# A fused attention and expert-FFN layer: the LoRA rows' transposes move one tile later, and a small product of the shared LoRA takes rounded operands

## What is computed

```
xn  = layernorm(x)
Q,K = elu(xn @ wq.T + bq) + 1, elu(xn @ wk.T + bk) + 1;  V = xn @ wv.T + bv      (16 heads of 32)
att = (Q @ (K^T V)) / (Q . sum(K) + 1e-8) @ wo.T + bo                            (linear attention)
w   = two best of 8 experts by sigmoid(xn @ W_router) + expert_bias, normalised
gate, up = xn @ W + (xn @ sA) @ sB / 8 + sum over experts of w_e (xn @ A_e) @ B_e / 8
hidden   = silu(gate) * up                                                        (1376 wide)
out = x + att + hidden @ W_down + (hidden @ sA_down) @ sB_down / 8 + experts' down LoRA
```

## Time and profile before

| | |
|---|---|
| median of the runs | 669.27 us |
| the profiled execution: its time, its span | 669.42 us, 667.6 us |
| PE matmuls busy | 659.3 us (99%) |
| DVE / ACT / POOL busy | 56% / 39% / 19% |
| granted TensorE clock | 1.000 of full speed |
| chain that ended last, by engine | PE 94%, DVE 3%, DMA 1%, ACT 1% |

### The profile page before, as it was taken

One profiled execution on the slowest core, in us unless ns is written; L12 is line 12 of the kernel. 1 busy time (PEld: TensorE's weight loads), 2 busy tenths in 40 slices (PEclk: granted clock), 3 DMA queues, 4 the chain that ended last, 5 costly groups with the idle time before them and its releaser, 6 DMA issues.

```text
span 667.6 us, 10326 instructions
## 1 busy us (share of the span) xinstructions
PE 659.3 (99%) x3568; PEld 545.4 (82%) x3568; DVE 376.3 (56%) x698; ACT 257.8 (39%) x413; POOL 127.1 (19%) x290
## 2 busy tenths in 40 slices
PE   7999999999999999999999999999999999999998
PEld 6899998877767788888888888888888888888886
DVE  6677888778676955434355443445344326534433
ACT  5434444566326323332343333243233324333321
POOL 3565676627336320000000000000000000000000
PEclk9999999999999999999999999999999999999999
DMA  6876665743745669930025000021400001300001
GB/s 215 311 256 212 214 235 194 261 183 149 292 170 196 236 183 3 77 128 0 1 79 221 32 0 0 0 75 72 184 0 0 0 8 71 127 0 0 0 0 63
DMA packets 41643, 74.21 MB, mean 111 GB/s; under 512 B 19393, under 2 KB 20289, under 8 KB 39953
## 3 DMA queue, kind: packets, MB, share of 16 engines
q1 hardware_dynamic: 38672, 64.52, 34.2%
q10 hardware_dynamic: 2736, 9.05, 3.4%
q0 software_dynamic: 208, 0.30, 0.3%
HBM read 52.81 MB, written 21.04 MB: 111 GB/s over the span
## 4 chain that ended last, share of the span: by engine, by line
PE 94%; DVE 3%; DMA 1%; ACT 1%; issue 0%; POOL 0%; DVEq 0%; POOLq 0%
PE bank L1246 21%; PE bank L1248 21%; PE bank L1247 21%; PE bank L1491 18%; PE bank L1464 6%; DVE den L1092 2%; PE bank L1477 1%; PE bank L1475 1%; PE bank L1265 1%; PE bank L1277 1%; DMA w_raw<-in_wkT 1%; PE bank L1364 1%; PE bank L1502 1%; PE bank L1504 1%; PE bank L1286 0%
## 5 line engine op out<-in xcount | busy, mean ns | idle before, releaser
L1246 PE MATMUL bank<-x,up_h 128*128 128x512 f32 (+1 forms) x352 | 137.1, 389 | 0.2 <-DVE x3r L1057 0.2
L1247 PE MATMUL bank<-x,up_h 128*128 128x512 f32 (+1 forms) x352 | 137.0, 389 | 0.0
L1248 PE MATMUL bank<-x,up_l 128*128 128x512 f32 (+1 forms) x352 | 137.0, 389 | 0.0
L1183 DVE TENSOR_TENSOR hf<-bank,silu 128x512 f32<-128x512 f32 x44 | 30.4, 691 | 155.0 <-issue 135.3
L1491 PE MATMUL bank<-dn,hid_h 128*128 128x512 f32 x352 | 108.8, 390 | 0.0
L677 ACT ACTIVATE hid_h<-hf 128x512 fp32r<-128x512 f32 x44 | 27.8, 632 | 144.1 <-DVE hf L1183 144.1
L1246 PEld LDWEIGHTS bank<-x,up_h 128*128 128x128 f32 x352 | 66.1, 188 | 14.4 <-issue 0.7
L1491 PEld LDWEIGHTS bank<-dn,hid_h 128*128 128x128 f32 x352 | 65.8, 188 | 14.5 <-DVE res L1208 0.6
L1248 PEld LDWEIGHTS bank<-x,up_l 128*128 128x128 f32 x352 | 66.1, 188 | 13.8
L1247 PEld LDWEIGHTS bank<-x,up_h 128*128 128x128 f32 x352 | 66.1, 188 | 13.7
L888 DVE TENSOR_TENSOR up_l<-up_raw,up_h 128x1024 fp32r<-128x1024 f32 x44 | 55.0, 1250 | 28.1 <-ACT up_h L677 28.1
(11 more groups left out here) (166 smaller groups left out, 1082.9 us busy)
## 6 DMA issues: line engine op xcount, KB each, us to landing
x<-scr_x SPq DMA_DIRECT2D x7, 2048.0 KB, 8.5
up_raw<-in_ffn_up SPq DMA_DIRECT2D x11, 768.0 KB, 7.4
scr_x<-xt ACTq DMA_DIRECT2D x16, 512.0 KB, 4.7
xin<-in_x SPq DMA_DIRECT2D x16, 256.0 KB, 4.9
scr_z<-zt SPq DMA_DIRECT2D x16, 256.0 KB, 2.1
x3r<-in_x SPq DMA_DIRECT2D x16, 256.0 KB, 3.1
scr_att<-x3r SPq DMA_DIRECT2D x16, 256.0 KB, 2.8
z<-scr_z SPq DMA_DIRECT2D x4, 1024.0 KB, 4.8
```

Of the source, the lines that this page charges most:

```text
L1183: nc.vector.tensor_tensor(hf[:], ps_u[:], silu[:], ALU.mult).then_inc(h_done, 1)
L1246: nc.tensor.matmul(dst, lh, rh, start=start, stop=False, **kw)
L1247: nc.tensor.matmul(dst, lh, rl, start=False, stop=False, **kw)
L1248: return nc.tensor.matmul(dst, ll, rh, start=False, stop=stop, **kw)
```

## The change

1. LoRA transposes. PE's `lora_transposed(t-2)` at the end of tile t becomes `lora_transposed(t-3)` directly behind tile t's `transpose_tokens(t+1)` (in tile 15, which has none, behind k). ACT's `lora_out(t-3)` comes behind the rounding of va, before the wait for `zraw`; DVE's `lora_lo(t-3)` comes behind `kf`, before `normalise(t+2)`. Tile 15 does two: pair 12 in the new place, and pair 13 at its end as before. SP stores each pair one tile later, so the store of pair 12 moves behind `x3_load(1)` and the load of `sa_dn`. Four tiles instead of two stand unrolled before the loop.
2. shared_down. The host puts sA_down and sB_down three times into each strip of 32 rows (24 rows of data). ACT rounds both (128x384 and 128x512) between queries(0,(2,)) and queries(0,(3,)), DVE turns the rows of one copy of each into remainders with two masks, and PE multiplies the rounded operands in one float32r matmul per chunk (the three copies give h.h, l.h and h.l).
3. `sa_r` and `sb_r` lie where later data go, so SP's loads of the up weights 8 to 10 and ACT's first `split_up` wait for the last shared_down (`sh_ready` 11).

```diff
 tiles:
-            body(0, 0, 0)
-            body(1, 0, 1)
-            with eng.Fori(0, SPLIT_FROM // 2 - 1) as p:
+            for t in range(4):
+                body(t, t // 2, t % 2)
+            with eng.Fori(2, SPLIT_FROM // 2) as p:
...
 SP:
             sp.dma_start(w_raw[:, 0], dram["woT"]).then_inc(s2_in, 16)
-            store_z(0)
...
             sp.dma_start(w_raw[:, 1], dram["wqT"]).then_inc(s2_in, 16)
-            store_z(1)
+            store_z(0)
...
                 if t < TILES - 1:
-                    store_z(t - 2)
+                    store_z(t - 3)
...
-            for t in range(TILES - 3, TILES - 1):
+            for t in range(TILES - 4, TILES - 1):
                 store_z(t)
...
             att_store(GROUPS - 2, True)
+            sp.wait_ge(sh_ready, FC)
             for c in range(WQ_CHUNK, FC):
 ACT:
                 round_to(vf[:, s, 0:KD - 1, :, 0:DK], ...).then_inc(va_done, 1)
+                if behind(t, 3):
+                    lora_out(t - 3)
...
-                if behind(t, 2):
+                if isinstance(t, int) and t == TILES - 1:
                     lora_out(t - 2)
...
-            queries(0, (2, 3))
+            queries(0, (2,))
+            act.wait_ge(sa_in, 16)
+            act.wait_ge(s2_in, 16 * STAGE2_LOADS)
+            act.wait_ge(vz_ready, TILES)
+            round_to(sa_r[:], sa_dn[:])
+            round_to(sb_r[:], sb_dn[:]).then_inc(shr_done, 1)
+            queries(0, (3,))
...
+            act.wait_ge(sh_ready, FC)
             split_up(0, 0, 0)
 DVE:
                 nc.vector.scalar_tensor_tensor(kf[:, s, :], ...).then_inc(kf_done, 1)
...
+                if behind(t, 3):
+                    lora_lo(t - 3)
                 if ahead(t, 2):
                     normalise(t + 2, s)
...
-                if behind(t, 2):
+                if isinstance(t, int) and t == TILES - 1:
                     lora_lo(t - 2)
...
             sub(bdn[0:ER, 1], bdn_raw[0:ER, 1], bdn[0:ER, 1]).then_inc(bdn_done, 1)
+            dve.wait_ge(shr_done, 1)
+            nc.vector.scalar_tensor_tensor(sa_r, sa_r, lomask[:, 1:2], sa_dn, ALU.mult, ALU.add)
+            nc.vector.scalar_tensor_tensor(sb_r, sb_r, lomask[:, 2:3], sb_dn, ALU.mult, ALU.add).then_inc(shl_done, 1)
             queries(0, (3,))
 PE:
                     transpose_tokens(t + 1)
+                if behind(t, 3):
+                    lora_transposed(t - 3)
...
-                if behind(t, 2):
+                if isinstance(t, int) and t == TILES - 1:
                     lora_transposed(t - 2)
...
-                pe.wait_ge(s2_in, 16 * STAGE2_LOADS)
-                pe.wait_ge(sa_in, 16)
+                pe.wait_ge(shl_done, 1)
...
-                    nc.tensor.matmul(ps_sh[c % SHG][:], sa_dn[strip, c // SHG, :], sb_dn[strip, :],
+                    nc.tensor.matmul(ps_sh[c % SHG][:], sa_r[strip, c // SHG, :], sb_r[strip, :],
```

More of the change, by code:

```diff
@@ L68 @@
     "ffn_up": (P, FC, UPC), "ffn_dn": (P, FC, DNC), "b_dn": (P, 2, D), "sa_dn": (P, SHN, P), "sb_dn": (P, D),
-    "ident": (P, P), "headmask": (P, HC), "headcol": (P, KD, DK), "lomask": (P, 1), "headrow": (P, P), "earlier": (1, E, E), "zmask": (P, 1),
+    "ident": (P, P), "headmask": (P, HC), "headcol": (P, KD, DK), "lomask": (P, 3), "headrow": (P, P), "earlier": (1, E, E), "zmask": (P, 1),
 }
@@ L92, in program @@
         nbq = sb("nbq", [P, KD])
-        lomask = sb("lomask_sb", [P, 1])
+        lomask = sb("lomask_sb", [P, 3])
         place = [-(-nc.sbuf_base // 32) * 32]
@@ L119, in program @@
         wq_l = at("wq_l", [P, KD, D], F32R)
+        sb_r = at("sb_r", [P, D], F32R)
         assert place[0] <= base
@@ L127, in program @@
         kvt_l = at("kvt_l", [P, KD, P], F32R)
+        sa_r = at("sa_r", [P, SHN, P], F32R)
+        assert place[0] <= wq_at + 4 * UPC
         place[0] = wq_at + 4 * UPC
@@ L312, in program @@
         sa_in = sem("sa_in")
+        shr_done = sem("shr_done")
+        shl_done = sem("shl_done")
         sh_ready = sem("sh_ready")
@@ L368, in tiles @@
         def tiles(eng, body):
-            body(0, 0, 0)
-            body(1, 0, 1)
-            with eng.Fori(0, SPLIT_FROM // 2 - 1) as p:
-                body(2 * p + 2, p + 1, 0)
-                body(2 * p + 3, p + 1, 1)
+            for t in range(4):
+                body(t, t // 2, t % 2)
+            with eng.Fori(2, SPLIT_FROM // 2) as p:
+                body(2 * p, p, 0)
+                body(2 * p + 1, p, 1)
             for t in range(SPLIT_FROM, TILES):
@@ L459, in _ @@
                 stage1(2 * p + 2, 0)
-                store_z(2 * p)
+                store_z(2 * p - 1)
                 x3a_load(p)
@@ L463, in _ @@
                 stage1(2 * p + 3, 1)
-                store_z(2 * p + 1)
+                store_z(2 * p)
                 load_dn(2 * p + 1)
@@ L1096, in reciprocal_lo @@
                 dve.wait_ge(rrh_done, g + 1)
-                nc.vector.scalar_tensor_tensor(rr[:], rr[:].bitcast(F32), lomask[:], den[:], ALU.mult, ALU.add
+                nc.vector.scalar_tensor_tensor(rr[:], rr[:].bitcast(F32), lomask[:, 0:1], den[:], ALU.mult, ALU.add
                                                ).then_inc(rr_done, 1)
@@ L1146, in _ @@
             sub(bdn[0:ER, 1], bdn_raw[0:ER, 1], bdn[0:ER, 1]).then_inc(bdn_done, 1)
+            dve.wait_ge(shr_done, 1)
+            nc.vector.scalar_tensor_tensor(sa_r[:].rearrange("p a n -> p (a n)"), sa_r[:].rearrange("p a n -> p (a n)").bitcast(F32),
+                                           lomask[:, 1:2], sa_dn[:].rearrange("p a n -> p (a n)"), ALU.mult, ALU.add)
+            nc.vector.scalar_tensor_tensor(sb_r[:], sb_r[:].bitcast(F32), lomask[:, 2:3], sb_dn[:], ALU.mult, ALU.add
+                                           ).then_inc(shl_done, 1)
             queries(0, (3,))
@@ L1584 @@
         rows = given["sA_down"][c * P:(c + 1) * P]
-        sa_dn[c % SHG * DK:c % SHG * DK + R, c // SHG, :rows.shape[0]] = rows.T
+        for j in range(3):
+            sa_dn[c % SHG * DK + j * R:c % SHG * DK + (j + 1) * R, c // SHG, :rows.shape[0]] = rows.T
     for i in range(SHG):
-        sb_dn[i * DK:i * DK + R] = given["sB_down"]
+        for j in range(3):
+            sb_dn[i * DK + j * R:i * DK + (j + 1) * R] = given["sB_down"]
     zmask = np.zeros((P, 1), f32)
@@ L1591 @@
     headcol = np.zeros((P, KD, DK), f32)
-    lomask = np.zeros((P, 1), f32)
+    lomask = np.zeros((P, 3), f32)
     headrow = np.zeros((P, P), f32)
@@ L1597 @@
         headrow[k * DK + h, c % P] = headrow[k * DK + LO + h, c % P] = 1.0
-    lomask[np.arange(P) % DK >= LO] = -1.0
+    lomask[np.arange(P) % DK >= LO, 0] = -1.0
+    lomask[np.arange(P) % DK // R == 1, 1] = -1.0
+    lomask[np.arange(P) % DK // R == 2, 2] = -1.0
     arrays = {
```

## The result

The changed kernel takes 673.39 us (median of 6 runs, 671.68 to 674.57) against 669.37 (6 runs, 669.05 to 669.83): ratio 1.0056 with a 95% interval of 1.0043 to 1.0068. It is slower by 4.0 us, where 1.7 were forecast, and outside the range of 668.0 to 672.8. The profiled execution took 674.12 us (span 672.3), 4.70 more than the one before.

What follows compares the result with a forecast made beforehand. PE, busy 659.3 of 667.6 us, was taken as the bound. +2.7 (waits ending stage 1, loop's 0.2 included) - 0.9 (shared_down) = +1.8 on 669.42 gives 671.2; median 0.15 lower, so 671.0 us, range 668.0 to 672.8.

Steps and rivals of the forecast that it cites:

- the second wait: End of stage 1: ACT's rounding of pair 13 awaits pair 12's store; kv_transposed(1) 2.7 us late, bounds 1.4 and 4.2.
- First wait: Tile 15: PE's transposes of pair 13 wait for DVE's lora_lo of pair 12, 1.1 us, called 1.0.
- the rival that kept only this wait: Pair 12's store slips past the load; only the tile 15 wait stays, +1.0 - 0.9: 669.4 us, 15 in 100.
- The store held by the load: End of stage 1: pair 12's store, issued behind the 2 MB load on SP, lands 1.15 us after it.
- The landing: Pair 12's store lands at 134.6, the load issued at 125.0 and landing at 133.5; bounds 133.3 and 136.1.
- The chain from ACT to pair 14 and to `kvm`: After ACT starts at 134.7: pair 14 transposed at 138.3 (1.58 + 1.91 + 0.1), kv_transposed(1) at 141.5 (1.58 + 5.10 + 0.1).
- Shared_down, -0.9: Stage 2: float32r strips take 0.78 us instead of 1.41; the three groups save 0.05, 0.65 and 0.2.
- Group 2: Stage 2, second group: denominators come at 192.6, just free of DVE's sums ending 192.49; saves 0.65 us (0.5 to 0.75).
- The loop, -0.2: Stage 1 loop: transposes put together save 0.02 us a tile, 0.2 over 13 tiles, already counted in the 2.7.
- The rival with 0.09 for each place: Places in the row of transposes are worth 0.09 us each and waits stay small: 667.2 us, 7 in 100.
- The roundings, nothing: ACT's roundings of `sa_r` and `sb_r` between the last two query blocks cost nothing, at most 0.3 us into denominators(0).
- the load runs long: Rival: load takes 10.0 us, ACT's slack is used up and the roundings show; +4.2 - 0.9: 672.6 us, 12 in 100.

Runs made afterwards that it cites:

- experiment 7: Changed kernel with the 2 MB load of x issued behind the stores of pairs 12 and 13 and sa_dn: 669.79 us (1.0012).
- experiment 8: experiment 7 plus a second PSUM bank, so pair 13's transposes no longer wait for pair 12's `zt`: 668.51 us (0.9988).
- Experiment 4: Kernel before the change, with only pair 12's store moved behind the 2 MB load: 673.67 us (1.0059).
- experiment 3: Changed kernel with pair 12's store issued ahead of the 2 MB load: 670.51 us (1.0014).
- experiment 5: Changed kernel with ten matmuls whose result nobody reads, on PE ahead of pair 14's transposes: 671.79 us (1.0037).
- experiment 6: Changed kernel with pair 12's store issued by ACT on its own queue instead of SP, at the same moment: 673.63 us (1.0056).
- experiment 2: Kernel before the change with the new float32r shared_down alone, LoRA pairs where they were: 668.66 us (0.9993).
- experiment 9: experiment 8 with denominators waiting only for the first of DVE's four shared_down sums: 667.52 us (0.9972).
- experiment 10: experiment 2 with denominators waiting only for the first of DVE's four shared_down sums: 667.60 us (0.9972).
- experiment 1: Changed kernel with shared_down as before (fp32), so only the LoRA transposes and stores move: 673.74 us (1.0060).

## Why the prediction was wrong

Direction and the chain of waits held: what was forecast to wait, waited, for the reason given. The failing step is the second wait, +2.7, which came to +5.52 at kv_transposed(1) (144.26 against 138.74). Two terms of it were wrong: the landing of the held store, 1.35 us too early, and PE's matmuls behind the wait, taken at full speed, where the halved clock cost 1.43. Either alone would have given about 672.5 us. Point by point:

- **First wait, "1.1 us, call it 1.0".** 1.19, with kf at 128.51 (forecast 128.2 to 128.5). Right, and inside the second wait in this kernel. Alone it costs 1.28 (experiments 7 and 8), so the rival that kept only this wait was priced 0.3 low.
- **The store held by the load, "1.15 after the load".** 1.1. Right. Experiment 4 shows it as the cause by itself.
- **The landing, "I put it at 134.6".** 135.98. The load was issued 0.27 later than I said and took 9.6 us where I took the median of its line, 8.5. ACT started 1.35 later than forecast (136.05 against 134.7). This was inside my bounds (136.1 was the upper end), so the term could be off by this much and still lie in the range. Landings of this load were 9.6, 9.7, 9.6 and 9.8 in four kernels with the transposes' new place and the load ahead, 8.9 in experiment 4, 8.2 in experiment 3.
- **The chain from ACT to pair 14 and to `kvm`, 3.59 and 6.78.** 3.59; `kvm` ended at 142.78, which is 6.73. Right.
- **What was not in the sum: the clock.** With `kvm` ready at 142.8, PE should have reached kv_transposed(1) there, +4.1, and in experiment 5 it did (142.77). It came at 144.26, because after its 2.07 us of idleness it worked at the 1.2 GHz level from 140.4 to 143.7. That is 1.43 us on this chain. The prediction said "all that follows hangs on PE from there" and took PE's own work behind the wait at its old duration. A wait of 1.2 us (experiments 3 and 7) brought no such loss; 2.07, 2.20 (experiment 6), 2.3 and 2.96 did, in the profiled runs.
- **Shared_down, -0.9.** -0.70 in the profile and -0.7 in experiment 2. The strips came at 0.78, as forecast; group 1 gave 0.0, with PE's wait at 0.87 (0.8 forecast); group 3 gave 0.23. Group 2 gave 0.47 and not 0.65: its sums now start at 195.57 and end at 198.04, and the denominators start at 198.30, 0.47 behind the last matmul (197.83) where it was 0.32 before (192.94 to 193.26). "Just free" was too hopeful; that step ran into DVE.
- **The loop, -0.2.** -0.10, and with the waits gone 0.08 (experiment 9 against 10). The 0.02 a tile was worked out from differences as small as the rounding of the rows. The rival with 0.09 for each place is out.
- **The roundings, nothing.** Right: ACT's two began at 146.14 and 146.56, and from kv_transposed(1) to denominators(0) it is 6.13 against 6.14.

The profiled execution adds up: 1.35 (ACT's start) + 0.04 (rounding of the 2.7) + 1.43 (clock) + 0.08 (shared_down and the tail) = 2.90, and 674.12 - 671.22 is 2.90. Of ACT's 1.35, about 0.3 is this run's late start. The first term lay within the bounds, the clock within none. The three runs with a mean clock of 0.999 or 1.0 took 671.7 to 672.8, 0.7 to 1.8 above the forecast.

I had asked of each wait how long it would be, and not what the engine that idled would do after it. The rival "the load runs long" had nearly the right landing (136.1) and still gave 672.6, for want of this term.

Open: why experiment 1 took up to 673.8 in runs with a mean clock of 0.999 and 1.0, about 1 us more than experiment 5's 671.79 and the 0.7 of shared_down make (the 0.82 that experiment 5's profiled run gained in group 1 could be most of it, if its other runs had it too, which is not recorded); how long PE's wait was in the runs whose clock did not fall, since only one run of each kernel was profiled; why this load took 0.7 to 0.9 us longer with the transposes in their new place than in experiment 4; and why one sixteenth of the load came so late (most of its 16 KB packets took 0.61 us each, a few 1.3 to 1.6).

## What to carry to other kernels

When a step is moved, list its DMAs too, and look at what large transfer each now stands behind: one 256 KB store issued after a 2 MB load, instead of ahead of it, cost this kernel 4.35 us by itself, and issuing it from another engine did not help. Price a new wait of TensorE as its length plus what the clock may take afterwards (here 1.4 to 1.7 us behind waits of 2 to 3 us, nothing behind 1.2), and if it can't be removed, give PE other work in it. And where a wait is for the last of several steps, ask which of them frees what is overwritten: that one line was worth 1.0 us, more than the part of the change that was meant to be quick.

## What the runs showed of the hardware

- TensorE idle for 2.07 us in a kernel otherwise at full clock: the granted clock stayed 1.00 until about 140.3, fell to half (0.42 us for 512 columns instead of 0.23) and came back at 143.7; these 3.3 us cost 1.43. With 2.40 us of matmuls in the same gap it stayed at 1.00. Other runs of the same kernel had a mean clock of 1.0; how long their wait was is not recorded, so whether a wait of this length always brings the fall is not shown.
- A 256 KB store took 2.1 us to land with no load before it. Issued 4.3 to 5.3 us behind a 2 MB load it took 5.7 to 6.0 on the load's own queue and 5.5 on ACT's, one to two microseconds of it for the last sixteenth of its bytes.
- The same DVE operation (two 128x512 fp32 tiles in SBUF added) took 0.68 us when it began in a gap of POOL's work and 1.76 to 1.79 when POOL was adding tiles of its own, in twelve profiled runs. In the one run with the short one, PE's wait of 0.87 us for DVE in that group was gone.
- Four float32r products on strips of 32 rows took 0.44 us to the next matmul's start (169.34 to 169.78), the same four in fp32 1.07 (163.84 to 164.91).
